# Linear attention on one Trainium2 core: the negative part of the feature map formed on ScalarE for every unit, VectorE's queue reordered, and the last four transposes in four PSUM banks

## The chip, the cores and the metric

The kernel runs on one core of a Trainium2 chip. The metric is the device time of one execution in microseconds (us); of several runs the median is given.

## The reference

The program is a decoder of two layers on x of 2 x 1024 tokens by 256 features. Each layer has a self-attention, a cross-attention to a short context and a feed-forward part. Only the self-attention of the second layer is touched here, a linear attention with 16 heads of 16:

```python
def _kernel_features(x, random_matrix):
    x_proj = jnp.einsum('bhsd,dm->bhsm', x, random_matrix)      # M = 64
    return (jax.nn.elu(x_proj) + 1.0) * INV_SQRT_M
...
q_prime = _kernel_features(q, random_matrix)
k_prime = _kernel_features(k, random_matrix)
kv = jnp.einsum('bhsm,bhsd->bhmd', k_prime, v)
k_sum = k_prime.sum(axis=2)
out = jnp.einsum('bhsm,bhmd->bhsd', q_prime, kv)
normalizer = jnp.maximum(jnp.einsum('bhsm,bhm->bhs', q_prime, k_sum)[..., None], 1e-06)
out = out / normalizer
```

The feature map elu(x) + 1 is max(x, 0) + exp(min(x, 0)).

## The kernel before

The whole program is a chain of stages, each a block of its own with one written-out instruction queue for each engine; semaphores order the queues. The stage in question is `feature_attention` (lines 1208 to 1483). After it `project_out` transposes the result and multiplies it by the output weights.

The 2048 tokens are 16 tiles of 128 (NT = 16), four tiles to a group (TPG = 4, NG = 4). The stage works in 32 units. Units 0 to 15 are key units (KU = 16), one for each token tile; units 16 to 31 are query units, four for each group, each with 4 of the 16 heads over 512 tokens. A unit is 128 x 1024 values in two PSUM banks: banks 0 and 1 for even units, 2 and 3 for odd ones. So TensorE may write unit n only when VectorE is done with unit n - 2.

TensorE's queue, for a key unit t: `key_features(t)` (line 1273), `values(t)` into bank 6 (line 1261), in two of four units a `project` of the next group into banks 4 and 5 (line 1254), and `key_value(t - 2)`, which adds to the sums in bank 7 (line 1288). For query unit i (q0 to q15): `query_features` (line 1315), in some a `project`, `mix_values` of unit i - 2 into bank 6 (line 1327), and `turn_mix(i - 7)`, four transposes into bank 7 (line 1336). Between the halves the key-value sums are copied, transposed (line 1353) and spread out (lines 1443 to 1450). The distance of 7 is LATE = TPG + 3. `turn_mix(t)` waits until `weight(t - 1)` has read bank 7.

ScalarE's queue, for each unit: `exponential`, then the projection copy `copy_proj` (line 1367), then for query units `copy_mix` of unit n - 2 (line 1385), which empties bank 6.

How the exponential of the negative part is formed depends on the unit. For odd units (`on_act`) ScalarE does both steps, relu(-x) out of PSUM (line 1373) and exp(-that) (line 1376). For even units VectorE first forms min(x, 0) (`lower`, line 1421) and ScalarE takes its exponential (line 1379). The result lies in `l_low`, which has three buffers.

VectorE's queue: `lower(n)` for even n, `copy_v(n)` (line 1438, which adds the bias to the values and empties bank 6), then `feature(n - 1)` (line 1433: max(x, 0) plus the exponential, in one instruction), and in the query half `weight(i - 8)`, three instructions (lines 1458, 1460 and 1462) that floor, invert and multiply. After the last unit the remaining `weight` calls follow one by one, each with its `turn_mix` in the same bank 7.

Of the kernel before, what the change touches and what calls it, by code (L numbers as in the profile page):

```python
# [17 lines left out]
ALU = mybir.AluOpType  # L18
ACT = mybir.ActivationFunctionType
AX = mybir.AxisListType.X  # L20

P = 128
# [5 lines left out]
NT = T // P  # L28
TPG = 4
NG = NT // TPG  # L30
G = TPG * P
QT = S // P
# [15 lines left out]
def wait(eng, sem, value):  # L48

    if isinstance(value, int) and value <= 0:  # L50
        return
    eng.wait_ge(sem, value)  # L52
# [1155 lines left out]
def feature_attention(k, attn, wq, wk, wv, operands):  # L1208
# [3 lines left out]
    own_sem, operands_done = k.sem("own"), k.sem("operands_done")  # L1212
    proj_ready, proj_done = k.sem("proj_ready"), k.sem("proj_done")
    v_ready, v_done = k.sem("v_ready"), k.sem("v_done")
    x_ready, low_ready, negated, exp_done, feat_done = (
        k.sem("x_ready"), k.sem("low_ready"), k.sem("negated"), k.sem("exp_done"), k.sem("feat_done"))
    kv_used, kv_copied, kv_turned, kv_done = k.sem("kv_used"), k.sem("kv_copied"), k.sem("kv_turned"), k.sem("kv_done")
    mixed, mix_copied, mix_turned = k.sem("mixed"), k.sem("mix_copied"), k.sem("mix_turned")
    floored, inverted, weighted = k.sem("floored"), k.sem("inverted"), k.sem("weighted")
    VW = 32  # L1220
# [2 lines left out]
    FLOOR = 1e-6 * 256.0  # L1223
    KU = NT
    QU = NG * TPG
    with ExitStack() as c, nc.Block() as block:
        bq_sb, bk_sb, bv_sb, r8 = operands
        mask4 = k.sb(c, "l_mask4", [P, 4])
# [5 lines left out]
        low = k.sb(c, "l_low", [P, 3, 2 * 512])  # L1234
# [4 lines left out]
        mix = k.sb(c, "l_mix", [P, 2, TPG, G])  # L1239
        den = k.sb(c, "l_den", [P, 2, H])  # L1240
        inv = k.sb(c, "l_inv", [P, 2, H])

        def on_act(n):

            return n % 2 == 1

        @block.tensor
        def _(pe):
# [47 lines left out]
            for t in range(NT):  # L1296
                g, j = divmod(t, TPG)
                key_features(t)
                values(t)
                if 1 <= j <= KD:  # L1300
                    n = KD * (g + 1) + j - 1
# [17 lines left out]
            def mix_values(n):  # L1319
                g, u = divmod(n - KU, TPG)  # L1320
                b, (kd, half) = g * TPG // QT, divmod(u, 2)
                pe.wait_ge(feat_done, n + 1)
                wait(pe, mix_copied, n - KU)
                if n == KU:
                    pe.wait_ge(kv_done, 1)
                for r in range(2 * half, 2 * half + 2):
                    last = pe.matmul(k.ps[64 * (r % 2):64 * (r % 2) + 64, 6, :], kv[:, b, kd, r, :], qp[:, g % 2, kd, r, :],
                                     start=True, stop=True)
                last.then_inc(mixed, 1)

            def turn_mix(t):
                g, q = divmod(t, TPG)
                pe.wait_ge(mix_copied, TPG * (g + 1))
                wait(pe, weighted, t)
                for u in range(TPG):
                    last = pe.transpose(k.ps[:, 7, u * P:(u + 1) * P], mix[:, g % 2, u, q * P:(q + 1) * P], k.ident[:, :])
                last.then_inc(mix_turned, 1)

            LATE = TPG + 3
            for n in range(KU, KU + QU + LATE):  # L1340
                i = n - KU
                if i < QU:
                    query_features(n)
                    g, u = divmod(i, TPG)
# [4 lines left out]
                if i == 1:  # L1349
                    pe.wait_ge(kv_copied, B)  # L1350
                    for b in range(B):
                        for kd in range(KD):
                            last = pe.transpose(k.ps[:, 6, (b * KD + kd) * P:(b * KD + kd + 1) * P], kvt[:, b, kd, :], k.ident[:, :])
                    last.then_inc(kv_turned, 1)
                if 2 <= i < QU + 2:
                    mix_values(n - 2)
                if i >= LATE:
                    turn_mix(i - LATE)

        @block.scalar  # L1360
        def _(act):
            def copy_proj(n):
                g, m = divmod(n, KD)
                act.wait_ge(proj_ready, n + 1)
                wait(act, x_ready, TPG * (g - 1))
                bias = bk_sb if g < NG else bq_sb
                act.activation(pj[:, g % 2, m, :], k.ps[:, 4 + m, :], ACT.Identity, bias=bias[:, m:m + 1]).then_inc(proj_done, 1)

            def exponential(n):
                if on_act(n):  # L1370
                    act.wait_ge(x_ready, n + 1)
                    wait(act, feat_done, n - 2)
                    act.activation(low[:, n % 3, :], k.ps[:, 2 * (n % 2):2 * (n % 2) + 2, :].rearrange("p a n -> p (a n)"),
                                   ACT.Relu, scale=-1.0).then_inc(negated, 1)
                    act.wait_ge(negated, n // 2 + 1)
                    act.activation(low[:, n % 3, :], low[:, n % 3, :], ACT.Exp, scale=-1.0).then_inc(exp_done, 1)
                else:
                    act.wait_ge(low_ready, n // 2 + 1)
                    act.activation(low[:, n % 3, :], low[:, n % 3, :], ACT.Exp).then_inc(exp_done, 1)

            def copy_mix(n):
                g, u = divmod(n - KU, TPG)
                act.wait_ge(mixed, n - KU + 1)
                wait(act, mix_turned, TPG * (g - 1))
                act.activation(mix[:, g % 2, u, :], k.ps[:, 6, :], ACT.Copy).then_inc(mix_copied, 1)

            for m in range(KD):
                copy_proj(m)
            for n in range(KU + QU + 2):
                if n < KU + QU:  # L1390
                    g, j = divmod(n, TPG)
                    exponential(n)
                    if n < KU and 1 <= j <= KD:
                        copy_proj(KD * (g + 1) + j - 1)
                    elif n >= KU and j < KD and g + 1 < 2 * NG:
                        copy_proj(KD * (g + 1) + j)
                if n >= KU + 2:
                    copy_mix(n - 2)

        @block.vector  # L1400
        def _(dve):
            own = Steps(dve, own_sem)
# [12 lines left out]
            def unit(n):  # L1415
                return k.ps[:, 2 * (n % 2):2 * (n % 2) + 2, :].rearrange("p a n -> p (a n)")

            def lower(n):
                dve.wait_ge(x_ready, n + 1)
                wait(dve, feat_done, n - 2)  # L1420
                dve.tensor_scalar(low[:, n % 3, :], unit(n), 0.0, None, ALU.min).then_inc(low_ready, 1)

            def feature(n):
                dve.wait_ge(exp_done, n + 1)
                if n < KU:
                    wait(dve, kv_used, n - 2)
                    dst = kp[:, n % 3, :, :, :, :].rearrange("p a k h m -> p (a k h m)")
                else:
                    g, u = divmod(n - KU, TPG)
                    kd, half = divmod(u, 2)  # L1430
                    wait(dve, mixed, TPG * (g - 1))
                    dst = qp[:, g % 2, kd, 2 * half:2 * half + 2, :].rearrange("p r n -> p (r n)")
                dve.scalar_tensor_tensor(out=dst, in0=unit(n), scalar=0.0, in1=low[:, n % 3, :],
                                         op0=ALU.max, op1=ALU.add).then_inc(feat_done, 1)

            def copy_v(t):
                dve.wait_ge(v_ready, t + 1)
                dve.tensor_tensor(va[:, t, :, 0:HD], k.ps[:, 6, 0:D].rearrange("p (h d) -> p h d", d=HD),
                                  bv_sb[:, :].rearrange("p (h d) -> p h d", d=HD), ALU.add).then_inc(v_done, 1)
# [14 lines left out]

            def weight(t):
                dve.wait_ge(mix_turned, t + 1)
                o = k.ps[:, 7, :].rearrange("p (h d) -> p h d", d=VW)
                dve.tensor_scalar(den[:, t % 2, :], o[:, :, HD], FLOOR, None, ALU.max).then_inc(floored, 1)
                dve.wait_ge(floored, t + 1)
                dve.reciprocal(inv[:, t % 2, :], den[:, t % 2, :]).then_inc(inverted, 1)  # L1460
                dve.wait_ge(inverted, t + 1)
                dve.tensor_tensor(attn[:, t, 0:D].rearrange("p (h d) -> p h d", d=HD), o[:, :, 0:HD],
                                  inv[:, t % 2, :].unsqueeze(2).to_broadcast([P, H, HD]), ALU.mult).then_inc(weighted, 1)

            LATE = TPG + 3
            for n in range(KU + QU + 1):
                if n < KU + QU and not on_act(n):
                    lower(n)
                if n < KU:
                    if n == 0:  # L1470
                        own.wait()
                    copy_v(n)
                if n >= 1:
                    feature(n - 1)
                if n == QT + 2:
                    copy_kv(0)
                if n == KU + 1:
                    copy_kv(1)
                    spread_kv()
                if n - KU > LATE:  # L1480
                    weight(n - KU - LATE - 1)
            for t in range(QU - LATE, NT):
                weight(t)


# [575 lines left out]
```

## Time and profile before

| | |
|---|---|
| Time, median of 3 runs | 1709.93 us (1709.0 to 1716.53) |
| The profiled execution's own time | 1718.02 us |
| Its span, first to last instruction | 1716.2 us |
| TensorE, VectorE, ScalarE busy over the span | 84%, 58%, 56% |
| Mean granted TensorE clock | 0.904 of full speed |

The profile covers one execution. Its own time is the one to set beside sums that are made from its rows; it is 8.1 us above the median of the runs. A busy share is an average over many stages with different limits, so the stage has to be read by itself: its first matmul starts at 955.8 us and its last weighting ends at 1114.3 us. The granted clock is given as a share of 2.4 GHz; in any moment of this trace it is either 1.00 or 0.50, and a value in between is a mean over a stretch.

### The profile page before, as it was taken

To read this page: it belongs to the slowest core of one execution; us is meant where nothing else is said; L and a number is where in the kernel's file an instruction comes from. 1 tells how busy PE (TensorE), PEld (TensorE's weight loads), DVE (VectorE), ACT (ScalarE), POOL (GpSimd) and SP (SyncE) were. 2 spreads that over 40 slices of the span, in tenths; PEclk is the share of its full clock that TensorE was granted. 3 is DMA by queue.
4 is the path that set the end of the run, shared out by engine and by line. 5 is a ranking of instruction groups with operands and counts; after the bars stand their busy time and mean duration, and the time that the engine had idled before them with its cause. 6 is when DMAs were issued, how large, how long until landed. Compare 5 with 4: busy or idle time off the path is not lost. (4 is left out here: it accounts for less than half of the span.)

```text
span 1716.2 us, 37930 instructions
## 1 busy us (share of the span) xinstructions
PE 1434.4 (84%) x12896; PEld 1036.1 (60%) x12899; DVE 997.3 (58%) x2203; ACT 955.9 (56%) x1897; POOL 162.3 (9%) x416
## 2 busy tenths in 40 slices
PE   5789999999999958998256788689997539999992
PEld 3257777777777755566014552265566339999992
DVE  5568888888888835544898654464544413333233
ACT  2479999999999913554473445234552013333330
POOL 0001111111111100002000000020002331111110
PEclk8889999999999979999558898799998569999997
DMA  4310000001001032000000000032002511111114
GB/s 131 121 36 25 22 28 26 20 27 28 21 24 28 11 124 78 1 1 4 15 0 19 12 2 0 1 143 89 1 4 72 177 64 37 37 37 37 35 35 156
DMA packets 59581, 74.28 MB, mean 43 GB/s; under 512 B 12804, under 2 KB 47276, under 8 KB 59500
## 3 DMA queue, kind: packets, MB, share of 16 engines
q1 hardware_dynamic: 52716, 56.63, 10.6%
q0 software_dynamic: 4672, 14.50, 2.5%
q10 hardware_dynamic: 2112, 2.10, 0.4%
q8 instruction: 48, 0.79, 0.2%
q14 instruction: 33, 0.27, 0.0%
HBM read 50.30 MB, written 22.88 MB: 43 GB/s over the span
## 5 line engine op out<-in xcount | busy, mean ns | idle before, releaser
L659 DVE CUSTOM_DVE_ANT_0 probs_sb<-banks,decay_sb 128x1024 f32<-128x1024 f32 x256 | 308.2, 1221 | 43.5 <-PE banks L578 22.4
L706 ACT ACTIVATE probs_sb<-probs_sb,shift_sb 128x1024 f32<-128x1024 f32 x256 | 294.7, 1151 | 18.0 <-POOL shift_sb L563 16.2
L588 PEld LDWEIGHTS banks<-ident_sb,probs_sb 128*128 128x128 f32 x2048 | 238.4, 141 | 55.0 <-issue 24.6
L588 PE MATMUL banks<-ident_sb,probs_sb 128*128 128x128 f32 x2048 | 267.8, 274 | 0.9 <-ACT probs_t_sb L521 0.8
L521 ACT ACTIVATE probs_t_sb<-banks 128x512 f32<-128x512 f32 x384 | 214.8, 597 | 4.1 <-PE banks L588 2.3
L578 PE MATMUL banks<-k_stack_sb,q_stack_sb 96*128 96x512 bf16 x512 | 156.9, 389 | 13.9 <-DMA k_stack_sb<-k_parts 10.7
L603 PE MATMUL banks<-probs_t_sb,v_head_sb 128*32 128x128 f32 x4096 | 151.2, 277 | 0.7 <-ACT probs_t_sb L521 0.7
L1743 PEld LDWEIGHTS banks<-slots_xt_sb,tile_w_sb 128*128 128x128 f32 x1248 | 146.2, 193 | 1.9
L1743 PE MATMUL banks<-slots_xt_sb,tile_w_sb 128*128 128x128 f32 x1248 | 146.4, 276 | 0.0
L1755 PE MATMUL banks<-experts_w_sb,xt_sb 128*128 x624 | 141.2, 379 | 1.3 <-issue 1.3
L1789 ACT ACTIVATE slots_xt_sb<-banks 128x256 f32<-128x256 f32 x39 | 15.0, 384 | 213.6 <-PE banks L1729 213.6
L1755 PEld LDWEIGHTS banks<-experts_w_sb,xt_sb 128*128 128x128 f32 x624 | 115.5, 190 | 15.8 <-issue 1.7
L519 DVE COPY probs_t_sb<-banks 128x512 f32<-128x512 f32 x128 | 88.6, 692 | 57.7 <-PE banks L588 56.0
L603 PEld LDWEIGHTS banks<-probs_t_sb,v_head_sb 128*32 128x32 f32 x4096 | 100.2, 109 | 32.3 <-issue 31.4
L884 DVE TENSOR_REDUCE peak_sb<-banks 128x8 f32<-128x616 f32 x64 | 51.2, 800 | 115.1 <-PE banks L795 115.1
L910 ACT ACTIVATE pt_sb<-banks 77x512 f32<-77x512 f32 x128 | 72.0, 591 | 81.5 <-PE banks L805 81.5
L794 PE MATMUL banks<-kbd_sb,qt_sb 128*128 128x308 f32 x256 | 94.8, 452 | 1.7 <-ACT qt_sb L921 1.7
L253 POOL TENSOR_TENSOR x_sb<-x_sb,bb_sb 128x256 f32<-128x256 f32 x48 | 33.0, 731 | 665.6 <-DMA bb_sb<-in_L_xattn_bo 354.7
L563 POOL TENSOR_TENSOR shift_sb<-peak_sb,minus_sb 128x1 f32<-128x1 f32 x256 | 49.1, 192 | 452.2 <-DVE peak_sb L659 452.2
L1799 ACT ACTIVATE xt_sb<-banks,tile_b_sb 128x128 f32<-128x128 f32 x312 | 84.9, 387 | 6.4 <-PE banks L1743 3.4
L1824 DVE TENSOR_TENSOR is_best_sb<-slots_x_sb,tile_owned_sb 128x1 f32<-128x1 f32 x39 | 6.2, 160 | 123.3 <-DMA outputs_y<-slots_y_sb,output_row_sb 122.7
L805 PE MATMUL banks<-ident_sb,pr_sb 128*77 128x128 f32 x512 | 76.7, 284 | 1.3 <-ACT pt_sb L910 1.3
(278 smaller groups left out, 2052.9 us busy)
## 6 DMA issues: line engine op xcount, KB each, us to landing
experts_w_sb<-in_L_ffn_W SPq DMA_DIRECT2D x16, 1024.0 KB, 12.0
q_stack_sb<-q_parts SPq DMA_DIRECT2D x192, 32.0 KB, 1.7
k_stack_sb<-k_parts SPq DMA_DIRECT2D x192, 32.0 KB, 1.8
slots_x<-zeros_sb POOLq DMA_DIRECT2D x1, 5031.0 KB, 21.2
slots_x_sb<-slots_x SPq DMA_DIRECT2D x39, 129.0 KB, 2.0
xt_sb<-outputs_y SPq DMA_DIRECT2D x8, 512.0 KB, 6.1
q_parts<-parts_sb SPq DMA_DIRECT2D x8, 384.0 KB, 3.0
k_parts<-parts_sb SPq DMA_DIRECT2D x8, 384.0 KB, 3.8
```

The costliest lines, as they stand in the source:

```text
L519: ins = eng.tensor_copy(dst, k.ps[:, 4 + half, :])
L521: ins = eng.activation(dst, k.ps[:, 4 + half, :], ACT.Copy)
L578: last = pe.matmul(k.ps[:, 2 * (s % 2) + half, :], qs[:, u, q * P:(q + 1) * P], ks[:, u, half * 512:(half + 1) * 512], start=True, stop=True)
L588: last = pe.transpose(k.ps[:, 4 + half, j * P:(j + 1) * P], pr[:, s % 4, (half * TPG + j) * P:(half * TPG + j + 1) * P], k.ident[:, :])
L603: last = pe.matmul(k.ps[32 * j:32 * j + 32, 6, 0:P], vh[:, u, kt, :], pt[:, j, gs % 2, kt, :], start=kt == 0, stop=kt == QT - 1)
L659: dve.tensor_tensor_reduce(out=pr[:, s % 4, :], in0=scores, in1=decay[:, off:off + S], scale=1.0, scalar=-3.0e38, op0=ALU.mult, op1=ALU.ma ...
L706: act.activation(pr[:, s % 4, :], pr[:, s % 4, :], ACT.Exp, bias=shift[:, s % 8:s % 8 + 1], accum_out=sums[:, (s // TPG) % 4, s % 4:s % 4 ...
L794: pe.matmul(k.ps[:, a, 0:HB * C], qt[:, kd, t * P:(t + 1) * P], rhs, start=True, stop=False)
L805: last = pe.transpose(k.ps[0:C, 4 + n % 2, h * P:(h + 1) * P], pr[:, t % 3, a * HB + h, :], k.ident[:, :])
L1743: last = pe.matmul(k.ps[:, 2 * u + f // HALF, (f % HALF) * P:(f % HALF + 1) * P], w1[:, u, kd, f * P:(f + 1) * P], xst[:, u, kd, :], start ...
L1755: last = pe.matmul(k.ps[:, 6, s * D:(s + 1) * D], ht[:, s, f, :], r.w2[:, bass.ds(e, 1), f, :].rearrange("p a n -> p (a n)"), start=f == 0 ...
L1799: ins = act.activation(ht[:, s, f, :], k.ps[:, 2 * s + f // HALF, (f % HALF) * P:(f % HALF + 1) * P], ACT.Gelu_apprx_tanh, bias=b1[:, s, f ...
```

## The change

`exponential` treats every unit alike: relu(-x) on ScalarE, then the exponential. `lower`, its semaphore and `on_act` are gone. VectorE's queue is now `feature(n)`, `copy_v(n + 1)`, with `copy_v(0)` ahead of the loop, and `weight` one loop step earlier in number, so that `weight(i - 7)` stands behind `feature` of query unit i. The last four transposes (t = 12 to 15) go to banks 7, 0, 2 and 4 in turn, and of these only the first waits for the weighting before it.

```diff
+    LATE = TPG + 3
+    TAIL_BANKS = [7, 0, 2, 4]
...
-        def on_act(n):
-
-            return n % 2 == 1
+        def turn_bank(t):
+            return TAIL_BANKS[t % TPG] if t >= NT - TPG else 7
...
                 pe.wait_ge(mix_copied, TPG * (g + 1))
-                wait(pe, weighted, t)
+                if turn_bank(t) == 7:
+                    wait(pe, weighted, t)
                 for u in range(TPG):
-                    last = pe.transpose(k.ps[:, 7, u * P:(u + 1) * P], mix[:, g % 2, u, q * P:(q + 1) * P], k.ident[:, :])
+                    last = pe.transpose(k.ps[:, turn_bank(t), u * P:(u + 1) * P], mix[:, g % 2, u, q * P:(q + 1) * P], k.ident[:, :])
...
             def exponential(n):
-                if on_act(n):
-                    act.wait_ge(x_ready, n + 1)
-                    wait(act, feat_done, n - 2)
-                    act.activation(low[:, n % 3, :], k.ps[:, 2 * (n % 2):2 * (n % 2) + 2, :].rearrange("p a n -> p (a n)"),
-                                   ACT.Relu, scale=-1.0).then_inc(negated, 1)
-                    act.wait_ge(negated, n // 2 + 1)
-                    act.activation(low[:, n % 3, :], low[:, n % 3, :], ACT.Exp, scale=-1.0).then_inc(exp_done, 1)
-                else:
-                    act.wait_ge(low_ready, n // 2 + 1)
-                    act.activation(low[:, n % 3, :], low[:, n % 3, :], ACT.Exp).then_inc(exp_done, 1)
+                act.wait_ge(x_ready, n + 1)
+                wait(act, feat_done, n - 2)
+                act.activation(low[:, n % 3, :], k.ps[:, 2 * (n % 2):2 * (n % 2) + 2, :].rearrange("p a n -> p (a n)"),
+                               ACT.Relu, scale=-1.0).then_inc(negated, 1)
+                act.wait_ge(negated, n + 1)
+                act.activation(low[:, n % 3, :], low[:, n % 3, :], ACT.Exp, scale=-1.0).then_inc(exp_done, 1)
...
-            def lower(n):
-                dve.wait_ge(x_ready, n + 1)
-                wait(dve, feat_done, n - 2)
-                dve.tensor_scalar(low[:, n % 3, :], unit(n), 0.0, None, ALU.min).then_inc(low_ready, 1)
...
-                o = k.ps[:, 7, :].rearrange("p (h d) -> p h d", d=VW)
+                o = k.ps[:, turn_bank(t), :].rearrange("p (h d) -> p h d", d=VW)
...
-            LATE = TPG + 3
+            own.wait()
+            copy_v(0)
             for n in range(KU + QU + 1):
-                if n < KU + QU and not on_act(n):
-                    lower(n)
-                if n < KU:
-                    if n == 0:
-                        own.wait()
-                    copy_v(n)
-                if n >= 1:
-                    feature(n - 1)
-                if n == QT + 2:
+                if n < KU + QU:
+                    feature(n)
+                if n + 1 < KU:
+                    copy_v(n + 1)
+                if n == QT + 1:
                     copy_kv(0)
-                if n == KU + 1:
+                if n == KU:
                     copy_kv(1)
                     spread_kv()
-                if n - KU > LATE:
-                    weight(n - KU - LATE - 1)
-            for t in range(QU - LATE, NT):
+                if n - KU >= LATE:
+                    weight(n - KU - LATE)
+            for t in range(QU - LATE + 1, NT):
                 weight(t)
```

## Rows read from the trace of the kernel before

**Rows 1.** Busy time by stretch, all engines; then granted clock, DMA share and GB/s.
```profile
955.80:1026.00 70.20, 60.23 (x682) 36.63 (x682) 38.70 (x51) 33.16 (x35) 0.00 (x0) 1.00 0.01 1
1026.00:1114.30 88.30, 68.50 (x284) 23.92 (x284) 44.25 (x76) 37.33 (x46) 0.00 (x0) 0.83 0.00 1
1039.80:1049.30 9.50, 9.50 (x18) 2.27 (x16) 3.57 (x3) 4.31 (x5) 0.00 (x0) 0.50 0.00 0
```

**Rows 2.** Waits between 957 and 1114 us: total us, times, longest.
```profile
ACT l_low_sb L1379 <- DVE l_low_sb L1421: 40.3, 16, 3.9
...
PE banks L1336 <- DVE attn_sb L1462: 13.6, 10, 2.4
```

**Rows 3.** Order of time on TensorE in the key half: start, length, instruction, idle before.
```profile
987.56 0.65 PE L1288 MATMUL banks<-l_kp_sb,l_va_sb 128*32 128x64 f32 x32
988.15 1.13 PE L1273 MATMUL banks<-l_rbd_sb,l_pj_sb 64*128 64x256 f32 x8
...
990.27 0.65 PE L1288 MATMUL banks<-l_kp_sb,l_va_sb 128*32 128x64 f32 x32
992.08 1.13 PE L1273 MATMUL banks<-l_rbd_sb,l_pj_sb 64*128 64x256 f32 x8 [1.16 <-DVE l_kp_sb L1433]
```

**Rows 4.** The same stretch on ScalarE, then on VectorE.
```profile
989.33 1.02 ACT L1373 ACTIVATE l_low_sb<-banks 128x1024 f32<-128x1024 f32 x1 [0.97 <-PE banks L1273]
990.38 1.06 ACT L1376 ACTIVATE l_low_sb<-l_low_sb 128x1024 f32<-128x1024 f32 x1
...
990.38 0.42 DVE L1438 TENSOR_TENSOR l_va_sb<-banks,l_bv_sb 128x256 f32<-128x256 f32 x1 [2.79 <-PE banks L1261]
990.72 1.21 DVE L1433 SCALAR_TENSOR_TENSOR l_kp_sb<-banks,l_low_sb 128x1024 f32<-128x1024 f32 x1
```

**Rows 5.** Order of time on TensorE in the query half.
```profile
1064.63 1.13 PE L1315 MATMUL banks<-l_pj_sb,l_rbd_sb 32*128 32x512 f32 x4
1065.69 1.98 PE L1254 MATMUL banks<-xt_sb,L_attn_Wq_sb 128*128 128x512 f32 x4
1067.61 1.08 PE L1327 MATMUL banks<-l_qp_sb,l_kv_sb 128*64 128x512 f32 x4
1068.62 0.66 PE L1336 MATMUL banks<-ident_sb,l_mix_sb 128*128 128x128 f32 x4
1069.20 1.13 PE L1315 MATMUL banks<-l_pj_sb,l_rbd_sb 32*128 32x512 f32 x4
...
1073.70 1.08 PE L1336 MATMUL banks<-ident_sb,l_mix_sb 128*128 128x128 f32 x4 [2.37 <-DVE attn_sb L1462]
```

**Rows 6.** Order of time at the start of the stage.
```profile
960.24 1.28 ACT L1379 ACT_TABLE_LOAD   x1
...
967.02 1.14 PE L1273 MATMUL banks<-l_rbd_sb,l_pj_sb 64*128 64x256 f32 x8
```

**Rows 7.** Groups by line (mean ns), then VectorE in order of time.
```profile
L1421 DVE TENSOR_SCALAR l_low_sb<-banks 128x1024 f32<-128x1024 f32 x16 | 19.6, 1224 | 41.1 <-PE banks L1315 30.2 <-PE banks L1273 10.6 <-DVE l_kv_sb L1450 0.2
...
L1385 ACT ACTIVATE l_mix_sb<-banks 128x512 f32<-128x512 f32 x16 | 9.4, 588 | 8.5 <-PE banks L1327 4.5 <-PE banks L1336 3.9
...
1063.02 0.17 DVE L1458 TENSOR_SCALAR l_den_sb<-banks 128x16 f32<-128x16 f32 x1
...
1063.85 1.21 DVE L1433 SCALAR_TENSOR_TENSOR l_qp_sb<-banks,l_low_sb 128x1024 f32<-128x1024 f32 x1
```

**Rows 8.** TensorE at the hand-over: q0, and q3 after the spreading.
```profile
1025.98 1.13 PE L1315 MATMUL banks<-l_pj_sb,l_rbd_sb 32*128 32x512 f32 x4 [1.16 <-DVE l_kp_sb L1433]
...
1038.46 1.43 PE L1315 MATMUL banks<-l_pj_sb,l_rbd_sb 32*128 32x512 f32 x4 [1.35 <-DVE l_qp_sb L1433]
```

**Rows 9.** Order of time in the tail: two turns, the last weighting.
```profile
1104.40 0.63 PE L1336 MATMUL banks<-ident_sb,l_mix_sb 128*128 128x128 f32 x4 [1.10 <-DVE attn_sb L1462]
...
1110.06 1.09 PE L1336 MATMUL banks<-ident_sb,l_mix_sb 128*128 128x128 f32 x4 [1.10 <-DVE attn_sb L1462]
...
1113.87 0.42 DVE L1462 TENSOR_TENSOR attn_sb<-banks,l_inv_sb 128x256 f32<-128x256 f32 x1
```

More of the change, by code:

```diff
@@ L1214, in feature_attention @@
     v_ready, v_done = k.sem("v_ready"), k.sem("v_done")
-    x_ready, low_ready, negated, exp_done, feat_done = (
-        k.sem("x_ready"), k.sem("low_ready"), k.sem("negated"), k.sem("exp_done"), k.sem("feat_done"))
+    x_ready, negated, exp_done, feat_done = (
+        k.sem("x_ready"), k.sem("negated"), k.sem("exp_done"), k.sem("feat_done"))
     kv_used, kv_copied, kv_turned, kv_done = k.sem("kv_used"), k.sem("kv_copied"), k.sem("kv_turned"), k.sem("kv_done")
@@ L1463, in weight @@
                                   inv[:, t % 2, :].unsqueeze(2).to_broadcast([P, H, HD]), ALU.mult).then_inc(weighted, 1)
-            LATE = TPG + 3
+            own.wait()
+            copy_v(0)
             for n in range(KU + QU + 1):
-                if n < KU + QU and not on_act(n):
-                    lower(n)
-                if n < KU:
-                    if n == 0:
-                        own.wait()
-                    copy_v(n)
-                if n >= 1:
-                    feature(n - 1)
-                if n == QT + 2:
+                if n < KU + QU:
[3 more added lines that the diff above has]
+                if n == QT + 1:
                     copy_kv(0)
-                if n == KU + 1:
+                if n == KU:
                     copy_kv(1)
                     spread_kv()
-                if n - KU > LATE:
-                    weight(n - KU - LATE - 1)
-            for t in range(QU - LATE, NT):
+                if n - KU >= LATE:
+                    weight(n - KU - LATE)
+            for t in range(QU - LATE + 1, NT):
                 weight(t)
```

## The prediction

> I name positions by the running number of a unit: key units 0 to 15, query units 16 to 31, q0 to q15 for the latter alone.
>
> **What bounds the kernel now.** First the busy shares by stretch: the stage runs from 955.8 to 1114.3 us. In its key half TensorE is busy for 60.2 of 70.2 us at full clock, VectorE for 38.7 and ScalarE for 33.2; in its query half TensorE is busy for 68.5 of 88.3 us, but at a mean granted clock of 0.83 [rows 1]. So TensorE is the engine nearest to its limit, and it loses time in two ways: about 30 us of idle, and stretches at the lower of its two levels (1.2 instead of 2.4 GHz), one of which, at a clock of 0.50, stands in [rows 1] too. From 0.83 over 88.3 us follow about 88.3 x 0.17 / 0.5 = 30 us at the lower level.
> Second the waits: ScalarE waited 40.3 us for VectorE's minimum, in 16 places, and TensorE waited 13.6 us for VectorE's `weight` before a `turn_mix` [rows 2]. The first number alone costs nothing, since ScalarE isn't the bound; what matters is whom the late minimum delays.
> Third the order of time shows it. In the key half a step without projection has 2.72 us of TensorE work: 2.12 from the start of the features at 988.15 to the key-value product at 990.27, and 0.59 for that product (987.56 to 988.15). The step takes 3.93, because TensorE sits idle for 1.16 until VectorE's `feature` of the unit before ends [rows 3]. That `feature` starts at 990.72, behind `copy_v` at 990.38, which itself had to wait for this step's values product [rows 4]. The exponential that it needs was long finished. So the queue order on VectorE is the cause, as much as the minimum. In the query half the same thing is larger: a `turn_mix` at 1073.70 comes after 2.37 us of idle, waiting for the `weight` that stands behind minimum and feature [rows 5]. The clock falls at about that moment.
>
> **The change part by part.**
> *Start.* VectorE's minimum of unit 0 had to follow two memsets. Now ScalarE's relu can start when its table load has run or, if the load is placed between relu and exponential, before it. Taking the late placement: relu from 961.55 (where the load of 1.28 us now ends [rows 6]), 1.02 for relu, 1.28 load, 1.06 exponential, feature from 964.9, 1.21, and 0.15 for the semaphore: the features of unit 2 start at 966.25 instead of 967.02 [rows 6]. Minus 0.8. The early placement ends within 0.3 of it, because TensorE is then busy with the projection until about 966.
> *Key half.* 16 minima of 1.22 us leave VectorE over both halves [rows 7], 16 relus of 1.02 come to ScalarE. The order on VectorE becomes feature(n), copy_v(n+1). New chain of a unit, from the start of its features on TensorE: relu at +1.18 (988.15 to 989.33), exponential at +2.23, feature at about +3.3, next user of the banks at +3.3 + 1.36 = +4.7 [rows 3, 4]. It may take two steps, and the shortest two hold 5.44 us of TensorE work: it hides. ScalarE needs 1.05 + 1.06 a unit, plus a projection copy of 0.69 in two of four, under 2.8 on average against TensorE's 3.6. So the key steps become bound by TensorE alone. Steps with a projection already are. Seven without one (3 to 4, 4 to 5, 7 to 8, 8 to 9, 11 to 12, 12 to 13, 15 to 16) shrink from 3.93 to 2.72: minus 8.5. q0 then starts at 1016.7 instead of 1025.98 [rows 8].
> *Hand-over.* The key-value transposes, the two spreading copies and their waits stay. Only the minimum in front of the feature of unit 17 goes: the idle 1.35 before 1038.46 [rows 8] nearly vanishes. q3 starts 11.2 after q0 instead of 12.5: minus 1.3.
> *Query half.* At full clock one step has features 1.06, mixing 1.01, turn 0.58, and a projection of 1.92 in some [rows 5]; a mix copy on ScalarE is 0.59 [rows 7]. I lay the queues side by side. ScalarE without projection: 1.05 + 1.0 + 0.6 = 2.65 a step, just TensorE's own 2.65. Two couplings bind in such steps: mixing waits for the mix copy that stands behind the exponential (3.9 after the features of the step before), and the turn waits for `weight` behind that step's feature: 3.3 + 1.2 + 0.9 = 5.4, then 0.6 of turn, for two steps. They give 2.9 a step instead of 2.65. In steps with a projection (4.57) nothing but TensorE binds. From q3 to q15: 12 x 1.06 + 4 x 1.92 + 12 x 1.01 + 8 x 0.58 = 37.1, plus 2.2 of such waits: 39.3. q15 starts at 1016.7 + 11.2 + 39.3 = 1067.2.
> *Tail.* From the start of q15: its feature ends at +4.5, weight(8) ends at +5.4, then turns 9 to 12 still share bank 7 and cost 1.73 each, the 0.63 of a turn and 1.10 of waiting [rows 9]: turn 12 starts at +10.5. Turns 13 to 15 follow in other banks without waiting; VectorE's `weight` is then the pace, 0.83 each back to back (1063.02 to 1063.85 [rows 7]). The last ends at about +14.6, at 1081.8. At half clock the four turns take 1.02 each and end 1.0 later; I take this, as the tail fell to the lower level in the trace (a turn of 1.09 [rows 9]). The stage ends at 1082.8 against 1114.3: minus 31.5. For four banks I had no row: if the turns went no faster than now, they'd give back 3 us; if all is as laid out and at full clock, one more is won.
> *The clock.* Of the 31.5, 0.8 + 8.5 + 1.3 = 10.6 come before q3. The rest, 21, is idle and low clock in the query half: the 30 us at the low level cost up to half of that, 15, where TensorE was the bound, I reckon 12 to 13; the other 8 or 9 are waits and tail. I assume that the clock stays up. In the key half it stayed at 1.00 with idles of 1.16 in every second step [rows 1, 3]; it fell in the query half around idles of 1.35 after others, and of 2.37 [rows 5, 8]; mine are 0.8 at most until the tail.
> *A rule against it.* The relu takes 1.02 us on ScalarE, and the two-operand VectorE step on the same banks 1.21 [rows 4], so VectorE isn't the quicker engine for this shape. The Trainium skill, page "ScalarE: Activation LUTs", section "Rules for kernel authors", says to put relu and min on VectorE, up to about 3 times faster in bf16. Here operands are fp32 in PSUM and the row disagrees. By the rule the removed minimum would be worth only a third of 1.02, some 0.34 us a unit by this estimate, and the sum would still be the same, since the key steps gain by the order on VectorE and not by its load.
>
> **The sum.** The profiled execution took 1718.0 us with a span of 1716.2; minus 31.5 gives 1686.5 for a like execution. The median, 1709.9, is 8.1 lower; minus 31.5 gives 1678.4. Part of those 8 may be low-clock time which the change takes away too, so I say 1679.
>
> **Rivals.**
> *A. The clock goes on falling as now.* The 30 us at the low level stay and cost those 12 to 13 beyond my sum: gain 19, 1691. For it: the bank waits remain, TensorE still has to wait at the hand-over for copy and spreading, and its query matmuls fill only 32 rows or 64 columns. Against: from 1064.63 to 1069.20 the same matmuls, back to back, ran at the upper level with no pause [rows 5], and in the new layout nearly all steps look like that. The Trainium skill's page "TensorE: Matmul & The Clock Gate", section "A second HAM failure mode: psum-queue depth-cycling", describes just such an oscillation from short idles while PSUM banks are cycled; by it this rival holds. 15%.
> *B. The change doesn't reach TensorE.* If ScalarE's longer queue took over the delay (mix copy behind relu and exponential), steps would keep their present 3.93 and the query half its length, and only the start and the turns would gain: 5 us, 1705. Against: ScalarE is busy for under half of the stage. 4%.
> *C. The other side: the low level for good.* If the clock falls at the hand-over and stays down, TensorE's work from q3 on takes twice its 1.06, 1.92, 1.01 and 0.58: 13 x 2.1 + 4 x 3.8 + 15 x 2.0 + 16 x 1.1 = 90 us in place of 55, and the gain turns into a loss of 3.5: 1713. If it falls already at unit 3, the 46 us from there to q0 double as well: 1759. It decides from some 64 us at that level (31.5 x 2), and reads slower by 0.5% from some 81. Against: the low stretch of [rows 1] ended by itself, and the key half had none at all. 2%.
> Mine, with the clock up but for the tail, 79%.
>
> **How the numbers follow.** A measurement of this kernel can tell about 0.5% (8.5 us) from no change. Mine and A lie below 1701, B and the milder half of C within 0.5%. Faster 0.94, same 0.05, slower 0.01. Range: 1671 (full clock in the tail too, and all of the 8 us still there to lose) to 1694 (A, with 3 us of couplings that I missed); outside lie B, C and luck of the later stages, together less than 2 in 10.
>
> **What would show it.** In the profile after: the stage near 127 us long; key steps without projection at 2.7 with no idle before the features; granted clock 1.00 from the start to the last turns; ScalarE waits for TensorE only; unprojected query steps at 2.9; turns 13 to 15 back to back and `weight` every 0.83. Low-clock stretches would mean A; features waiting for ScalarE's exponential would mean B. The rest of the program should take what it takes now; a difference there would make the total wrong with the stage right.

## The result and the profile after

| | before | changed |
|---|---|---|
| Median (4 runs each) | 1712.49 us (1709.0 to 1716.53) | 1687.12 us (1682.1 to 1691.56) |
| Ratio, 95% interval | | 0.985 (0.9807 to 0.9894) |
| Profiled span | 1716.2 us | 1680.3 us |
| The stage, first matmul to last weighting | 955.8 to 1114.3: 158.5 | 952.4 to 1078.4: 126.0 |
| From the stage's end to the end of the span | 601.9 | 601.9 |

The kernel became faster by 1.5%. A second measurement on another occasion (experiment e0_after) gave 0.9827 (0.9806 to 0.9848), 1685.4 beside 1715.0 us. In the profiles the stage lost 32.5 us; another 3.4 us had gone before it began, in stages that the change doesn't touch.

Busy time by stretch of the changed kernel, the same view as [rows 1]: key half, query half, then its middle from q3 to q15, and the tail.

```profile
952.41:1012.86 60.45, 59.58 (x680) 36.31 (x680) 31.13 (x43) 40.65 (x43) 0.00 (x0) 1.00 0.01 2
1012.86:1078.37 65.51, 56.16 (x291) 20.34 (x284) 35.30 (x68) 45.46 (x55) 0.00 (x0) 1.00 0.00 1
...
1024.12:1063.60 39.48, 37.45 (x145) 12.11 (x145) 20.18 (x33) 32.94 (x41) 0.00 (x0) 1.00 0.00 0
1063.60:1077.80 14.20, 8.74 (x49) 4.35 (x48) 9.10 (x28) 4.88 (x7) 0.00 (x0) 1.00 0.01 2
```

TensorE is now busy for 59.6 of 60.5 us in the key half, and the clock is 1.00 in every stretch; in [rows 1] the query half had 0.83.

The waits in the changed kernel, as in [rows 2]; `feature` is line 1425 here, the relu 1373, the exponential 1376, the turns 1338, the weighting 1450 to 1454:

```profile
DVE l_qp_sb L1425 <- ACT l_low_sb L1376: 21.4, 15, 2.8
...
DVE l_kp_sb L1425 <- ACT l_low_sb L1376: 11.2, 16, 1.7
...
PE banks L1338 <- DVE attn_sb L1454: 4.3, 6, 1.1
```

VectorE now waits for ScalarE. Most of that costs nothing, because VectorE is not the bound; only in query steps without projection does it delay the weighting that a turn needs, as shown below. TensorE's wait for the weighting fell from 13.6 to 4.3 us. Behind the start of the stage, TensorE's wait for `feature` in the key half is gone, as its order of time shows beside [rows 3]:

```profile
967.34 1.14 PE L1274 MATMUL banks<-l_rbd_sb,l_pj_sb 64*128 64x256 f32 x8
968.41 1.13 PE L1262 MATMUL banks<-L_attn_Wv_sb,xt_sb 128*128 128x256 f32 x4
969.47 0.65 PE L1289 MATMUL banks<-l_kp_sb,l_va_sb 128*32 128x64 f32 x32
970.05 1.13 PE L1274 MATMUL banks<-l_rbd_sb,l_pj_sb 64*128 64x256 f32 x8
```

A step is 2.71 us with no idle. At the start, as in [rows 6], the table load has moved behind the first relu:

```profile
958.12 1.02 ACT L1373 ACTIVATE l_low_sb<-banks 128x1024 f32<-128x1024 f32 x1 [1.32 <-PE banks L1274]
...
959.16 1.28 ACT L1376 ACT_TABLE_LOAD   x1
...
962.92 1.13 PE L1274 MATMUL banks<-l_rbd_sb,l_pj_sb 64*128 64x256 f32 x8
```

In the last group the coupling that is left shows: in every second step TensorE sits idle for 0.52 us before a turn, until the weighting is done. The first of the last four turns still waits 1.11 for bank 7; then their sixteen transposes run in one piece, and the weightings, 0.82 apart, are the pace (compare [rows 9]):

```profile
1063.04 0.63 PE L1338 MATMUL banks<-ident_sb,l_mix_sb 128*128 128x128 f32 x4
...
1066.46 0.63 PE L1338 MATMUL banks<-ident_sb,l_mix_sb 128*128 128x128 f32 x4 [0.52 <-DVE attn_sb L1454]
...
1074.32 1.94 PE L1338 MATMUL banks<-ident_sb,l_mix_sb 128*128 128x128 f32 x16 [1.11 <-DVE attn_sb L1454]
...
1077.13 0.42 DVE L1454 TENSOR_TENSOR attn_sb<-banks,l_inv_sb 128x256 f32<-128x256 f32 x1
...
1077.95 0.42 DVE L1454 TENSOR_TENSOR attn_sb<-banks,l_inv_sb 128x256 f32<-128x256 f32 x1
```

### The profile page after: what moved, and what is told of

The parts are those of the page before. It is cut to its first block and busy times, and to the rows that moved or that the text cites. A ratio compares the mean times of both kernels' runs of the same rounds, so it can differ in the third digit from the quotient of the medians.

```text
span 1680.3 us, 37928 instructions
## 1 busy us (share of the span) xinstructions
PE 1418.5 (84%) x12898; PEld 1029.9 (61%) x12899; DVE 979.8 (58%) x2187; ACT 971.5 (58%) x1913; POOL 162.0 (10%) x416
## 5 line engine op out<-in xcount | busy, mean ns | idle before, releaser
L1744 PEld LDWEIGHTS banks<-experts_w_sb,xt_sb 128*128 128x128 f32 x624 | 115.5, 190 | 15.8 <-issue 1.7
L1828 DVE COPY tile_w_sb<-experts_w_sb 128x2048 f32 x39 | 47.8, 1227 | 61.4 <-issue 27.4
```

What stands on the lines that cost most here:

```text
L1744: last = pe.matmul(k.ps[:, 6, s * D:(s + 1) * D], ht[:, s, f, :], r.w2[:, bass.ds(e, 1), f, :].rearrange("p a n -> p (a n)"), start=f == 0 ...
```

## The experiments

Stage lengths below are from the first matmul of the stage to the end of the last weighting, each in one profiled execution.

### One part at a time: e1_order, e2_relu, e3_tail

Three kernels, each the kernel before with one part of the change.

e1_order, VectorE's order alone:

```diff
-                if n < KU:
-                    if n == 0:
-                        own.wait()
-                    copy_v(n)
                 if n >= 1:
                     feature(n - 1)
+                if n < KU:
+                    if n == 0:
+                        own.wait()
+                    copy_v(n)
```

> The kernel before, with one edit: on VectorE feature(n-1) stands ahead of copy_v(n). Minima stay where they were. My theory (the queue order on VectorE holds TensorE in the key half as much as the minimum): in key steps whose unit is odd (n = 3, 7, 11, 15) feature(n-1) no longer waits for the values product, and the step without projection falls from 3.93 to 2.72 us; in even ones (4, 8, 12) the minimum still stands ahead, features of the next unit can start 3.65 after this one's, and the step falls to 3.65. Key half shorter by 4 x 1.2 + 3 x 0.3 = 5.7 us; query half as before, since copy_v has no part in it. Total about 6 us shorter (0.996). Rival (the minimum alone is the cause): key steps keep 3.93, no change.

Measured: 0.997 (0.9953 to 0.9987), 1710.9 beside 1715.0 us. The key half took 64.3 us instead of 70.2, minus 5.9. TensorE's order of time, then VectorE's, for an odd unit's step and the start of an even one's:

```profile
969.91 1.13 PE L1273 MATMUL banks<-l_rbd_sb,l_pj_sb 64*128 64x256 f32 x8
...
972.62 1.13 PE L1273 MATMUL banks<-l_rbd_sb,l_pj_sb 64*128 64x256 f32 x8
...
973.80 1.22 DVE L1421 TENSOR_SCALAR l_low_sb<-banks 128x1024 f32<-128x1024 f32 x1 [1.23 <-PE banks L1273]
...
974.94 1.21 DVE L1433 SCALAR_TENSOR_TENSOR l_kp_sb<-banks,l_low_sb 128x1024 f32<-128x1024 f32 x1
```

The step of the odd unit is 2.71 (3.93 before); in the even one `feature` starts only behind the minimum, and that step measured 3.59 (3.65 expected). The order on VectorE holds TensorE by itself, and the minimum does so in even units alone. The query half took 88.0 us, beside 88.3 in the profile of the kernel before.

e2_relu, the relu alone: `exponential` as in the changed kernel, `lower` removed, VectorE's order and the turns as before:

```diff
...
-                if n < KU + QU and not on_act(n):
-                    lower(n)
                 if n < KU:
```

> The kernel before with the minima moved and nothing else: ScalarE forms relu and exponential of every unit, VectorE keeps its old order copy_v(n), feature(n-1), and the last turns stay in bank 7. My theory: key steps without projection keep 3.93 us, because feature(n-1) still stands behind copy_v(n), which ends 2.57 after the features' start, plus 1.21 and 0.15; of the key half only the start gains, 0.8. The query half has no copy_v and gains in full: hand-over 1.3, waits and clock some 17, so the stage is 19 to 20 us shorter (0.988) and the granted clock is 1.00 up to the tail. Rival (the minimum is the whole cause): key steps at 2.72 too, stage 28 us shorter. Rival A of the prediction (clock goes on falling): low-clock stretches in the query half, stage some 8 us shorter.

Measured: 0.991 (0.9891 to 0.993), 1699.2 us; the stage 138.8 us, 19.6 shorter. Two stretches, key and query half, and a key step:

```profile
956.62:1025.81 69.19, 60.15 (x681) 36.60 (x681) 30.00 (x44) 41.24 (x43) 0.00 (x0) 1.00 0.01 1
1025.81:1095.45 69.64, 58.15 (x284) 21.18 (x284) 35.36 (x68) 44.88 (x54) 0.00 (x0) 0.94 0.00 1
```

```profile
990.42 0.42 DVE L1434 TENSOR_TENSOR l_va_sb<-banks,l_bv_sb 128x256 f32<-128x256 f32 x1 [2.87 <-PE banks L1261]
...
990.76 1.21 DVE L1429 SCALAR_TENSOR_TENSOR l_kp_sb<-banks,l_low_sb 128x1024 f32<-128x1024 f32 x1
992.12 1.14 PE L1273 MATMUL banks<-l_rbd_sb,l_pj_sb 64*128 64x256 f32 x8 [1.16 <-DVE l_kp_sb L1429]
```

With no minimum left on VectorE, the key half still waits 1.16 us, just as in [rows 3], and gains 1.0 us only. All the rest came in the query half, whose time from q0 to q15 is 50.7 us, the changed kernel's own, at a clock of 1.00. The 0.94 of the whole query half comes from the tail: from q15 to the end it takes 18.9 us as before, at a mean clock of 0.80, and its turns slow down from 0.65 to 1.09 us between pauses of 1.10:

```profile
1087.27 0.65 PE L1336 MATMUL banks<-ident_sb,l_mix_sb 128*128 128x128 f32 x4 [1.10 <-DVE attn_sb L1458]
1089.02 1.09 PE L1336 MATMUL banks<-ident_sb,l_mix_sb 128*128 128x128 f32 x4 [1.10 <-DVE attn_sb L1458]
```

So the relu pays in the query half and the order in the key half, and there only with the relu in place: by itself the order gave 5.9 us, on top of the relu it gives 8.7 (69.2 down to 60.5). The medians give the relu 15.8 us (1715.0 to 1699.2) where the profiles give 19.6; why a profile of the kernel before can overstate a gain is taken up under r_before.

e3_tail, the four banks alone:

```diff
...
-                wait(pe, weighted, t)
+                if turn_bank(t) == 7:
+                    wait(pe, weighted, t)
...
```

> The kernel before with one edit: the last four turns in banks 7, 0, 2 and 4, of which only the first waits for the weighting before. My theory: the turns 13 to 15 take 0.83 to 1.05 each in place of 1.73 to 2.19, the stage is 3 to 4 us shorter and nothing else moves; 0.998, at the edge of what 5 rounds can tell, so the profile decides. Rival: a weighting that reads one bank while transposes write another is slowed, or the end is bound by the weighting anyway: no gain.

Measured: 0.9977 (0.9958 to 0.9995). From q15 to the end of the stage 15.0 us instead of 18.9, minus 3.9: no slowing of a weighting beside transposes into another bank. The sixteen transposes ran at the lower level there (3.26 us in place of 1.94 in the changed kernel), and the stretch was still only 0.2 us longer than the changed kernel's 14.8:

```profile
1098.80 3.26 PE L1342 MATMUL banks<-ident_sb,l_mix_sb 128*128 128x128 f32 x16 [1.11 <-DVE attn_sb L1468]
```

The stage was 151.8 us, 6.7 shorter, which is more than the edit: from q0 to q15 it took 66.6 us instead of 69.4, with the same instructions. That difference is taken up under r_before.

### The same two kernels once more: e0_after, r_before

e0_after is the changed kernel, r_before the kernel before, both unedited.

> The changed kernel again, beside the kernel before on one chip. The stage gained 32.5 us in the two profiles, but the medians lie 25 us apart. Theory 1 (sampling: four runs a side that spread over 8 us): here the ratio is 0.981 to 0.982, 31 to 33 us. Theory 2 (the profiled execution of before had more low-clock time in this stage than its usual one): the ratio stays at 0.985, and a profile of the unedited stage on this chip would show it. In the profile of this run the stage is again 126 us long at a clock of 1.00, or else it has low stretches now and then.

> The kernel before once more, for a second profile of it. Theory 2 of the run of the changed kernel (low-clock time in this stage differs from execution to execution before the change): the stage is not 158.5 us again, but between 152 and 159, and the difference sits in low-clock stretches of the query half; the key half is again 70.2. Theory 1 (the spread comes from other stages): the stage is 158 to 159 again, and stage start or the rest of the program differ by some us.

Measured: e0_after 0.9827 (0.9806 to 0.9848), 29.6 us between the medians, its stage 126.0 us at clock 1.00 again. r_before: one time of 1712.4 us, its stage 152.7 us. Key half, then query half of r_before:

```profile
955.83:1025.99 70.16, 60.22 (x681) 36.59 (x681) 38.69 (x51) 33.14 (x35) 0.00 (x0) 1.00 0.01 1
1025.99:1108.51 82.52, 62.82 (x284) 22.39 (x284) 44.03 (x76) 37.31 (x46) 0.00 (x0) 0.90 0.00 1
```

The key half repeats to 0.01 us; the query half is 5.8 us shorter than in [rows 1] at a clock of 0.90 instead of 0.83. By the same arithmetic as in the prediction, 82.5 x 0.10 / 0.5 = 16.5 us were spent at the lower level in place of 30. So before the change this stage had no one length: it fell from 158.5 to 152.7 with nothing edited, and the gain is 26.7 or 32.5 us by which one is taken; 29.6 lies between them. From q0 to q15 four profiles have the same instructions and lengths from 63.7 to 69.4 us, the 66.6 of e3_tail among them. In order: before, e1_order, e3_tail, r_before:

```profile
1025.98:1095.42 69.44, 57.94 (x236) 18.78 (x237) 35.11 (x48) 32.97 (x40) 0.00 (x0) 0.83 0.00 0
1018.58:1087.71 69.13, 58.15 (x244) 18.97 (x237) 35.12 (x48) 33.68 (x41) 0.00 (x0) 0.83 0.00 0
1021.45:1088.03 66.58, 55.15 (x237) 17.77 (x237) 35.02 (x48) 32.96 (x40) 0.00 (x0) 0.87 0.00 0
1025.99:1089.64 63.65, 52.23 (x236) 17.22 (x236) 34.91 (x48) 32.96 (x40) 0.00 (x0) 0.92 0.00 1
```

The same arithmetic gives 23.6, 23.5, 17.3 and 10.2 us at the lower level, and the lengths follow it at about 0.42 us for each of these us. With the mean of the four, 67.2, the stage before is some 156.3 us and the gain some 30, by this estimate, close to the 29.6 between the medians.

Theory 2 of r_before, low-clock time that differs between executions, is borne out. The ratio of e0_after alone decides little: 0.9827 lies between what its two theories gave (0.981 to 0.982, and 0.985). Other stages have their part as well: the eight profiles of these experiments begin the stage between 951.3 and 957.2 us and need 600.4 to 604.5 us after it, with unchanged code on both sides. Together that is 1552.7 to 1561.1 us outside the stage, a difference of 8.4 us between profiles; the runs of one kernel spread over 5 to 12 us.

### The other assignment: e4_all_min

The changed kernel with every minimum on VectorE:

```diff
...
-                act.activation(low[:, n % 3, :], k.ps[:, 2 * (n % 2):2 * (n % 2) + 2, :].rearrange("p a n -> p (a n)"),
-                               ACT.Relu, scale=-1.0).then_inc(negated, 1)
...
-            own.wait()
-            copy_v(0)
             for n in range(KU + QU + 1):
                 if n < KU + QU:
-                    feature(n)
-                if n + 1 < KU:
-                    copy_v(n + 1)
+                    lower(n)
+                if n >= 1:
+                    feature(n - 1)
+                if n < KU:
+                    copy_v(n)
...
```

VectorE's order is that of e1_order, so the edit moves `feature` and the weightings back by one loop step as well: beside e1_order it moves the odd units' minima to VectorE and gives the last turns their four banks.

> The changed kernel with the minima of all 32 units on VectorE and only the exponential on ScalarE; VectorE's order is lower(n), feature(n-1), copy_v(n), and the last four turns keep their own banks. My theory (a minimum on VectorE stands ahead of the feature and the weighting that TensorE waits for): key steps without projection 3.6 us (2.71 in the changed kernel), key half 66.6 us; query steps with a turn 4.95 (VectorE: minimum from 1.1 after the features' start, feature, weighting, then 0.6 of turn), query half to the last features 67 us against 50.7; the stage 150 us at full clock, up to 156 with falls of the clock, for which idles of 2.3 us give occasion. Rival (the Trainium skill, page 'ScalarE: Activation LUTs', section 'Rules for kernel authors': minimum and relu belong on VectorE): the minimum is quick there and the stage is no longer than the changed kernel's 126 us.

Measured: 1716.9 us, 1.0018 (1.0007 to 1.0029) of the kernel before. The stage took 164.6 us: the key half 68.4 (1.7 over my figure, mainly a later start and the step in which key-value sums are copied), from q0 to q15 77.1, where I had 67. Beside e1_order the key half is 4.1 us longer and the way from q0 to q15 7.9. The query half, and one of its steps:

```profile
1023.68:1119.89 96.21, 77.26 (x284) 26.80 (x284) 53.44 (x85) 29.26 (x38) 0.00 (x0) 0.72 0.00 1
```

```profile
1094.27 2.08 PE L1316 MATMUL banks<-l_pj_sb,l_rbd_sb 32*128 32x512 f32 x4
...
1096.40 1.22 DVE L1414 TENSOR_SCALAR l_low_sb<-banks 128x1024 f32<-128x1024 f32 x1 [3.29 <-PE banks L1316]
1097.54 1.22 DVE L1426 SCALAR_TENSOR_TENSOR l_qp_sb<-banks,l_low_sb 128x1024 f32<-128x1024 f32 x1
...
1099.73 1.08 PE L1338 MATMUL banks<-ident_sb,l_mix_sb 128*128 128x128 f32 x4 [1.47 <-DVE attn_sb L1455]
1100.74 2.08 PE L1316 MATMUL banks<-l_pj_sb,l_rbd_sb 32*128 32x512 f32 x4
```

About 54 us were spent at the lower level (96.2 x 0.28 / 0.5). There the features themselves take 2.0 us and stand in the chain, so a step that I had at 4.95 takes 6.47. I had allowed 6 us for the clock; behind q0 the stage is 12.8 us above my sum at full clock, most of which I put down to it. The rival rule of the Trainium skill ("ScalarE: Activation LUTs", section "Rules for kernel authors"), whose figure is for bf16, doesn't hold for this shape: the minimum of 128 x 1024 fp32 from PSUM took 1.22 us on VectorE, the relu 1.02 on ScalarE, and with the minima on VectorE the kernel's median was some 31 us above the changed one's in e0_after. The 0.2 us between the two instructions, over 32 units, is 6.4 us at most; the rest I put down to where the minimum stands in VectorE's queue, and to the clock.

### The new bound doubled: e5_relu_twice

```diff
...
+                if n >= KU:
+                    act.activation(low[:, n % 3, :], k.ps[:, 2 * (n % 2):2 * (n % 2) + 2, :].rearrange("p a n -> p (a n)"),
+                                   ACT.Relu, scale=-1.0).then_inc(once, 1)
+                    act.wait_ge(once, n - KU + 1)
                 act.activation(low[:, n % 3, :], k.ps[:, 2 * (n % 2):2 * (n % 2) + 2, :].rearrange("p a n -> p (a n)"),
                                ACT.Relu, scale=-1.0).then_inc(negated, 1)
```

> The changed kernel with the relu of each query unit done twice on ScalarE (same operands, same result): the suspected new bound doubled. My theory: ScalarE then needs 3.7 us in a query step without projection (2.1 relu, 1.0 exponential, 0.6 mix copy) and becomes the bound there; steps with projection keep 4.57. The stage is 8 to 9 us longer, 135. TensorE's idle in these steps is 1.0 of 3.7 us; theory clock-by-idle says that the granted clock may now fall in the last group, which would cost up to 5 more; if it stays 1.00 there, idles of 1.0 don't bring it down. Rival (ScalarE still has slack in the changed kernel): the second relu hides, stage 126 to 128.

Measured: one time of 1696.0 us, the stage 141.6 us, 15.7 longer than the changed kernel's, the key half as there (60.5). TensorE in steps without projection:

```profile
1034.58 1.13 PE L1317 MATMUL banks<-l_pj_sb,l_rbd_sb 32*128 32x512 f32 x4
1037.39 1.08 PE L1329 MATMUL banks<-l_qp_sb,l_kv_sb 128*64 128x512 f32 x4 [1.68 <-ACT l_mix_sb L1387]
1038.40 2.08 PE L1317 MATMUL banks<-l_pj_sb,l_rbd_sb 32*128 32x512 f32 x4
...
1060.28 1.08 PE L1329 MATMUL banks<-l_qp_sb,l_kv_sb 128*64 128x512 f32 x4 [1.19 <-ACT l_mix_sb L1387]
1061.88 0.73 PE L1339 MATMUL banks<-ident_sb,l_mix_sb 128*128 128x128 f32 x4 [0.52 <-DVE attn_sb L1459]
1062.54 2.08 PE L1317 MATMUL banks<-l_pj_sb,l_rbd_sb 32*128 32x512 f32 x4
```

TensorE waits for the mix copy behind the doubled relu, and the step is 3.82 us at full clock (3.7 expected). So ScalarE has no slack when such steps follow each other; the first one behind two steps with a projection (1055.31 to 1057.96) still took 2.65. The rest is the clock: right behind both places the features take 2.08 instead of 1.13 us. The query half's granted clock was 0.83, as in the kernel before; I put the 6.6 us above my 135 down to it. What brings the clock down is thus not tied to the minimum: here there is none on VectorE, TensorE waits for ScalarE instead, and the falls are back.

### More banks: e6_banks

```diff
         def turn_bank(t):
-            return TAIL_BANKS[t % TPG] if t >= NT - TPG else 7
+            if t >= NT - TPG:
+                return t - (NT - TPG)
+            return 4 if t >= 5 and t % 2 == 1 else 7
+
+        def turn_needs(t):
+            return 0 if t >= NT - TPG else (t if t < 5 else t - 1)
+
+        def mix_bank(m):
+            return 5 if m >= 10 and m % 2 == 1 else 6
+
+        def mix_needs(m):
+            return m if m < 11 else m - 1
...
```

> The changed kernel with more PSUM banks for the couplings that are left: once the projections are done (from q12 on) turns alternate between banks 7 and 4 and mixed values between banks 6 and 5, each waiting for the reader but one; the last four turns go to banks 0 to 3 and wait for no weighting. My theory: the last group's steps fall from 3.04 on average to 2.65 (minus 1.5 us), and turns 9 to 12 no longer cost 1.73 each, so that after q15 VectorE's eight weightings at 0.83 set the end: 11.2 us instead of 14.8. Stage 121 us, 5 shorter; ratio to the kernel before 0.980, that is 0.003 under the changed kernel's, at the edge of what rounds tell, so the profile decides. Rival (the tail is bound by the mixing and its copies): no more than 2 us.

Measured: 0.9794 (0.9774 to 0.9813), 1678.0 us; the stage 121.8 us, 4.2 under the changed kernel's. Three starts of features in the last group, and the query half:

```profile
1058.94 1.13 PE L1327 MATMUL banks<-l_pj_sb,l_rbd_sb 32*128 32x512 f32 x4
...
1061.59 1.13 PE L1327 MATMUL banks<-l_pj_sb,l_rbd_sb 32*128 32x512 f32 x4
...
1064.24 1.13 PE L1327 MATMUL banks<-l_pj_sb,l_rbd_sb 32*128 32x512 f32 x4
```

```profile
1014.28:1075.59 61.31, 55.66 (x291) 20.28 (x284) 35.00 (x68) 45.46 (x55) 0.00 (x0) 1.00 0.00 1
```

The steps are 2.65, TensorE's own work, and from q15 to the end it is 11.4 us (11.2 expected) instead of 14.8. The steps of the last group gave 0.8 us back where I had 1.5. The ratio's interval meets that of e0_after at its edge, so that this is faster than the changed kernel rests on the stage's length more than on the ratio. It is the fastest version here.

## Why the prediction was right, point by point

*Start.* 0.8 expected; unit 2's features began 10.5 us after the stage's first matmul instead of 11.2. The load came late, as I had assumed.

*Key half.* Seven steps of 2.72 expected, 2.71 measured. q0 came 60.5 us after the first matmul, where I had 60.9: I had left out the step in which the first key-value sums are copied; it fell from 4.93 to 4.42. e1_order and e2_relu show that the queue order was worth 5.9 us by itself, the relu 1.0, and that only both together give 9.7.

*Hand-over.* q3 expected 11.2 after q0, measured 11.26.

*Query half.* q3 to q15: 39.3 expected, 39.5 measured. The two couplings are there: before the mixing one pause of 0.72 and two of some 0.2, before two of the turns 0.52. They come in every second step (3.42 beside 2.65) and not evenly, as my 2.9 a step had it.

*Tail.* 14.6 expected, 14.8 measured, but at full clock; the 1.0 that I added for the lower level did not come. It was also too large: in e3_tail the four turns did run at the lower level, and the tail took 15.0, 0.2 more, since the weightings on VectorE are the pace there.

*The clock.* It stayed at 1.00 throughout the stage in all three profiles with these queues (the changed kernel twice, e6_banks), so rival A failed. The profile was needed for that: the time alone, 1687.1, lies nearer to A's 1691 than to my 1679. e5_relu_twice ties the falls to TensorE's waits, because doubled work on ScalarE brought both back together. ScalarE's load as such is not the cause: from q0 to q15 e2_relu had it busy for 40.0 of 50.7 us at 1.00, the kernel before for 33.0 of 69.4 at 0.83. Which property of a wait brings a fall stays open. My 12 to 13 us for the clock were for 30 us at the lower level; the 0.42 us of r_before's four profiles gives about 10 for the 23.6 of them that lay between q0 and q15, and in the tail three turns took 2.19 each at the lower level in place of 1.73, 1.4 more. So the clock was worth some 11 us, by this estimate, and of the 18.7 that q0 to q15 lost the other 9 were waits. r_before shows that the share varies by some 6 us from one execution to the next.

*The sum.* For the stage 31.5 were expected and 32.5 measured. What was off is the last step, the way from the profile to the median: I took the whole 31.5 from a median of 1709.9, allowing less than 1 us for low-clock time that this profile had above others. It had 5.8 more than r_before, and the median of three runs was itself low; the later ones were 1712.5, 1715.0 and 1714.5. The gain between medians was 25.4 and then 29.6, and the time 1687.1 where I had said 1679, inside the range.

*Rivals B and C.* ScalarE's longer queue did not take over the delay, but e5_relu_twice shows how near it is: one more microsecond on ScalarE a step, and TensorE waits. C's picture of a clock that stays down came in another kernel, and only in part: e4_all_min was at the lower level for 54 us, nearly all of the stretch from 1077.3 to 1112.3 among them, but it had risen twice before, and the kernel lost all that its queue order had won. In C's sum the 55 us are the length of the stretch with its waits; TensorE's own work there is 46.

## What to carry to other kernels

When a wait on another engine looks like the cause, read what stands ahead of the waiting instruction in its own queue too: here moving the minimum away gave 1.0 us in the key half until the feature stood ahead of the copy, and 9.7 then. Put an operation on the engine where nobody stands behind it, and price it from rows of the same shape, not by a rule about engines. Where the clock falls in a stage, take two profiles before pricing it, and treat what one profile shows of it as one sample.

## What the runs showed of the hardware that I had not expected

The granted clock doesn't simply follow how long TensorE is idle. In the key half of 70 us TensorE paused for up to 1.16 us in seven of sixteen steps, two by two, at 60.2 us busy, and the clock never left 1.00, in five profiles (both of the kernel before, e1_order at its shorter pauses, e2_relu, e3_tail): 2.3 us of pauses in two steps of 7.8 us together. In the query half of e5_relu_twice it fell behind one pause of 1.68, and behind pauses of 1.19 and 0.52 in one step, the step before which had none: 1.7 us of pauses in two steps of 7.2. The matmuls differ: in the key half they fill 64 or 128 rows (the key-value products 32 columns), in the query half the features fill 32 rows and the mixing 64 columns. That can't be the whole reason, since in the tail of e2_relu the clock fell between transposes that fill 128 rows and columns. The reason stays open.

The fall is also not the same from one execution to the next: with identical instructions before, the query half spent 30 us at the lower level in one profile and 16.5 in another.
